# A mixed attention and feed-forward chain on one core: a scaling and half of a rounding moved from DVE to ACT, and all four engines' orders planned anew

## Chip, cores and metric

One NeuronCore of a Trainium2 chip runs the whole program in one launch. The metric is the device time of one execution in microseconds; lower is better. Half a per cent, 1.6 us, is about what a measurement of this kernel can tell from no change.

## The reference

The input x has 2 sequences of 512 tokens with 128 features; the context has 77 tokens for each sequence. Four layers follow each other, and every one adds to x:

```python
x = x + tanh(g_xattn[0]) * xattn0(layernorm(x), ctx, mask)     # 16 heads of 8
x = x + tanh(g_ffn[0])   * relu_mlp(layernorm(x))              # 128 -> 512 -> 128
x = x + tanh(g_xattn[1]) * xattn1(layernorm(x), ctx)           # one key and value head
x = x + tanh(g_ffn[1])   * (top-2 of 16 experts + shared expert)(layernorm(x))
x = x + tanh(g_xattn[2]) * xattn2(layernorm(x), ctx)
x = x + tanh(g_ffn[2])   * (one of 32 experts)(layernorm(x))
x = x + tanh(g_xattn[3]) * slots3(layernorm(x), ctx)           # 3 passes of slot attention + GRU
x = x + tanh(g_ffn[3])   * int8_product(layernorm(x), rhs)
```

In slots3 each pass takes scores of the tokens against the 77 keys, a softmax over the tokens (so each key's row has a sum over 512 tokens), divides by the sum over the keys, multiplies by the values, and feeds a GRU cell. In the last product every token's row is scaled by 127 / max|row| and rounded to integers.

## The kernel before

The two sequences are called halves (b = 0 and 1); half 2 in the code is preparation of weights and keys that both share. The work is cut into some 850 steps: ("pe", "scores", 1, 2, 0) is TensorE's part of the scores of half 1, layer 2, chunk 0. A step of one phase runs on PE (TensorE), ACT (ScalarE), DVE (VectorE) or POOL (GpSimd), and its followers wait for it by semaphores. Half 0 runs ahead of half 1, so that one half's matmuls fill the time in which the other half waits for ACT or DVE.

The order of the steps on each engine is fixed before the launch. `schedule()` is a list planner: it takes, again and again, the step with the lowest rank, which is its earliest possible time by the step times written in `prepare_steps` and `half_steps`, plus an offset of its own from the table `LATER`, minus a share of the work that still hangs on it. The same planner deals out the 8 PSUM banks of 512 columns, and puts spare matmuls into gaps that it sees on PE (`IDLE_FILLERS`, function `keep_warm`, 0.22 us each; their product is never read). In rows these fillers are `psum<-halves 128x512` (early on `psum<-wide 128x512`). Both kernels start with 13 more of them.

Names that the steps of this text touch:

- Attention layers: `maxima` (PE products of 32 rows into 4 banks, then DVE `TENSOR_REDUCE mx`), `max_rows` (four transposes and an ACT copy to `mx_t`), `scores` (PE into 4 banks, three products in parts hi and lo and one with `mx_t`; then four ACT exponentials into `wide`), `sums` and `values` (products with 32 columns: `wide,heads_of` and `wide,v_cols`), `sum_rows`, `spread`, `project`.
- PE works in three ways: whole (128x128), rows (32 rows: `maxima`, `scores`) and columns (32 columns: `sums`, `values`). The planner counts 0.095 us where the way changes (`SWITCH`).
- Slot passes: `slots_turn`, `slot_products`, `slot_scores` (DVE maximum, then ACT exponential with its sum over tokens), `slot_inverse` (reciprocal of the sum, then 78x386 value rows times it), `gru` (four products `wide 78x386`, each followed by a DVE reciprocal L1857 and L1858), `gru_r`, `gru_z`, `gru_end` (L1864, L1865, L1870, L1874, L1875 on DVE; three tanh and an Identity on ACT), `hidden`.
- The end: `integers` (row maximum L1578, scale, reciprocal L1580, four roundings L1582), `turn` of stage 7 (transposes, ACT L1373, clipping L1891), `quantised` (L1898, L1902), and the output's DMA.

Two lines of the slot pass before:

```python
                link(V.reciprocal(nmax[0:CTX, b, 2:3], nmax[0:CTX, b, 1:2]))
                V.tensor_scalar(vw_s[0:KEYS, b, :], vw[0:KEYS, b, :], nmax[0:KEYS, b, 2:3], None, ALU.mult)\
```

Of the kernel before, what the change touches and what calls it, by code (L numbers as in the profile page):

```python
# [7 lines left out]
ALU = mybir.AluOpType  # L8
ACT = mybir.ActivationFunctionType
# [6 lines left out]
P = 128  # L16
# [3 lines left out]
T = S // P  # L20
# [121 lines left out]
def first_columns(name, k):  # L142
# [49 lines left out]
}  # L192


# [1825 lines left out]
```

## Time and profile before

| | |
|---|---|
| median of 3 runs | 322.0 us (321.52 to 323.16) |
| the profiled execution | 322.01 us |
| its span | 320.2 us |
| busy: PE, DVE, ACT, POOL | 302.7, 231.3, 140.5, 60.2 us |
| instructions: PE, DVE, ACT, POOL | 2118, 642, 294, 83 |
| shares of the chain that ended last | PE 71%, DVE 19%, ACT 7%, issue 2% |

The span runs from the first to the last instruction that the profile shows; 1.8 us of the execution lie around it. Busy time of PE holds the fillers too, so a full PE is not yet a PE that does useful work. A time in a row is counted from the span's start.

### The profile page before, as it was taken

The page shows a single profiled execution, that of the slowest core. Times are in us where ns is not written, and L with a number is a line of the kernel's source. Part 1 is how long each engine was busy: PE and PEld are TensorE (multiplying, and loading weights), DVE is VectorE, ACT ScalarE, POOL GpSimd, SP SyncE. Part 2 cuts the span into 40 slices and gives each one's busy share as a digit, 9 for nine tenths or more (in the row PEclk, how much of TensorE's full clock was granted, in tenths as well). Part 3 has the DMA queues.
Part 4 walks back from the last instruction along what each step waited for, and adds up shares of the span by engine and source line. Part 5 has one row for each costly group of instructions (what it writes and reads, how often), then busy time and mean ns, then how long its engine had stood idle before and what let it go on. Part 6 is the DMA issues. An engine that isn't in the chain of part 4 may idle for free.

```text
span 320.2 us, 5732 instructions
## 1 busy us (share of the span) xinstructions
PE 302.7 (95%) x2118; PEld 202.6 (63%) x2118; DVE 231.3 (72%) x642; ACT 140.5 (44%) x294; POOL 60.2 (19%) x83
## 2 busy tenths in 40 slices
PE   8899999998899999999999999999999998899983
PEld 3463553883445478888788356479879874676441
DVE  4996864779866486878776485376457668999995
ACT  1337365234547462342424637513335636666300
POOL 6217631344001001003030301010210401001210
PEclk9999999999999999999999999999999999999998
DMA  6950220003100000000000000000000000000002
GB/s 177 320 201 0 72 74 2 0 3 85 60 0 2 2 0 0 3 0 2 0 2 0 1 3 2 0 2 0 0 2 0 2 1 2 0 1 2 0 1 66
DMA packets 8976, 8.73 MB, mean 27 GB/s; under 512 B 3547, under 2 KB 6901, under 8 KB 8949
## 3 DMA queue, kind: packets, MB, share of 16 engines
q1 hardware_dynamic: 8949, 8.37, 8.8%
q8 instruction: 17, 0.28, 0.4%
q14 instruction: 10, 0.08, 0.1%
HBM read 7.84 MB, written 0.52 MB: 26 GB/s over the span
## 4 chain that ended last, share of the span: by engine, by line
PE 71%; DVE 19%; ACT 7%; issue 2%; DVEq 0%; ACTq 0%
PE psum L974 65%; DVE mx L1695 4%; DVE wide L1858 2%; PE psum L1065 2%; ACT wide L1373 1%; ACT wide L1511 1%; DVE xn L1568 1%; PE psum L1103 1%; DVE xn L1875 1%; DVE wide L1865 1%; PE psum L1159 1%; ACT q L1373 1%; DVE xn_t L1874 1%; DVE wide L1864 1%; ACT wide L1501 1%
## 5 line engine op out<-in xcount | busy, mean ns | idle before, releaser
L913 POOL TENSOR_TENSOR nw<-mv,minus_half 128x2 f32<-128x2 f32 x32 | 22.5, 716 | 157.3 <-DVE mv L1562 157.3
L1373 ACT ACTIVATE wide<-psum 128x512 f32<-128x512 f32 x72 | 36.9, 614 | 11.6 <-PE psum L974 11.5
L1695 DVE TENSOR_REDUCE mx<-psum 128x4 f32<-128x308 f32 x96 | 38.6, 471 | 4.5 <-PE psum L974 4.3
L1373 ACT ACTIVATE q<-psum 128x512 f32<-128x512 f32 (+1 forms) x36 | 21.0, 594 | 27.2 <-PE psum L974 19.1
L974 PE MATMUL psum<-q_hi,first_hi 128*128 128x512 f32 (+1 forms) x68 | 31.6, 464 | 0.0
L974 PE MATMUL psum<-halves 128*128 128x512 bf16 x123 | 30.5, 379 | 0.5 <-ACT wide L1373 0.5
L974 PE MATMUL psum<-wide 78*128 78x386 f32 (+1 forms) x70 | 25.7, 503 | 3.1 <-DVE wide L1846 1.5
L974 PE MATMUL psum<-q_hi,first_lo 128*128 128x512 f32 (+1 forms) x68 | 26.9, 395 | 0.0
L974 PE MATMUL psum<-q_lo,first_hi 128*128 128x512 f32 (+1 forms) x68 | 26.8, 394 | 0.0
L974 PEld LDWEIGHTS psum<-early,wide 128*128 128x128 f32 x192 | 24.2, 192 | 1.4 <-DVE wide L1858 0.2
L974 PE MATMUL psum<-early,wide 128*128 128x128 f32 x192 | 24.7, 276 | 0.0
L974 PEld LDWEIGHTS psum<-w_ffn,wide 128*128 128x128 f32 (+1 forms) x176 | 22.8, 191 | 1.9 <-issue 0.4
L974 PE MATMUL psum<-w_ffn,wide 128*128 128x128 f32 (+1 forms) x176 | 23.4, 276 | 0.0
L974 PE MATMUL psum<-w_attn,q 128*128 128x128 f32 x176 | 22.8, 278 | 0.1
L974 PEld LDWEIGHTS psum<-w_attn,q 128*128 128x128 f32 x176 | 21.1, 192 | 1.3 <-issue 0.6
L1568 DVE TENSOR_SCALAR xn<-x,mv,nw 128x128 f32<-128x128 f32 x64 | 19.3, 351 | 2.6 <-POOL nw L913 1.4
L974 PEld LDWEIGHTS psum<-halves 128*128 128x128 bf16 x123 | 11.7, 98 | 13.0 <-issue 3.0
L974 PE MATMUL psum<-wide,v_cols 128*32 128x512 f32 x144 | 18.9, 598 | 0.5 <-DVE mx L1695 0.5
L974 PEld LDWEIGHTS psum<-wide 78*128 78x128 f32 (+1 forms) x70 | 11.2, 170 | 12.5 <-issue 5.2
L974 PE MATMUL psum<-wide,heads_of 128*32 128x512 f32 x144 | 18.9, 602 | 0.1
L1770 DVE TENSOR_TENSOR wide<-q,psum 128x512 f32<-128x512 f32 (+1 forms) x22 | 14.6, 683 | 5.8 <-ACT q L1373 4.4
L1373 ACT ACTIVATE wide<-psum,cols 128x512 f32<-128x512 f32 x12 | 8.2, 686 | 22.9 <-PE psum L974 22.8
(230 smaller groups left out, 551.7 us busy)
## 6 DMA issues: line engine op xcount, KB each, us to landing
early<-in_ffn SPq DMA_DIRECT2D x8, 256.0 KB, 3.1
w_attn<-in_attn SPq DMA_DIRECT2D x1, 640.0 KB, 7.7
w_attn<-in_attn SPq DMA_DIRECT2D x2, 288.0 KB, 6.5
x<-in_x SPq DMA_DIRECT2D x2, 256.0 KB, 3.8
w_ffn<-in_ffn SPq DMA_DIRECT2D x1, 512.0 KB, 7.0
early<-in_ffn SPq DMA_DIRECT2D x1, 512.0 KB, 3.9
out<-x SPq DMA_DIRECT2D x2, 256.0 KB, 2.3
rows<-in_rows SPq DMA_DIRECT2D x1, 468.0 KB, 6.2
```

The costliest lines, as they stand in the source:

```text
L913: G.tensor_tensor(nw[:, b, 2, tiles], mv[:, b, tiles, 1], minus_half[:, tiles], ALU.pow)\
L974: return nc.tensor.matmul(out_, lhs, rhs, start=start, stop=stop, **kw)
L1065: last = nc.tensor.transpose(bk[:, t * P:(t + 1) * P], (y if stage == 7 else xn)[:, b, t, :], ident)
L1103: last = nc.tensor.transpose(bk[:, t * P:(t + 1) * P], mx[:, b, t, :], ident)
L1159: last = nc.tensor.transpose(bk[:, t * P:(t + 1) * P], rinv_d[:, b, t, :], ident)
L1373: A.activation(dst, banks.bank(*name)[0:rows_, 0:cols_], fn, **kw).then_inc(drained["act"], 1)
L1501: last = A.activation(sq[:, b, t, :], slots[:, b, t, :], ACT.Square, accum_out=nw[:, b, 1, t:t + 1])
L1511: A.activation(ex[0:CTX, b, :], banks.bank("s", it, b)[0:CTX, :], ACT.Exp, bias=nmax[0:CTX, b, 0:1], accum_out=nmax[0:CTX, b, 1:2]).then_i ...
L1568: last = V.tensor_scalar(xn[:, b, t, :], x[:, b, t, :], mv[:, b, t, 0:1], nw[:, b, 2, t:t + 1], ALU.subtract, ALU.mult)
L1695: last = V.tensor_reduce(mx[:, b, t, lane_heads(g)], banks.bank("max", layer, b, t, g)[:, 0:GK].rearrange("p (h k) -> p h k", k=CTX), AX.X ...
L1770: V.tensor_tensor(wide[0:r, b, at_, :], act_s[k % 2][0:r, b, :], banks.bank("up", b, k)[0:r, :], ALU.mult)\
L1858: V.scalar_tensor_tensor(gates[:, b, t, :], u[:, 0:3 * D], inverse, gates_h[:, b, t, :], ALU.mult, ALU.add)\
```

## The change

There are three parts, and nothing that is computed changes. First, in each of the three slot passes of each half DVE now makes only the reciprocal of the sums; the product of the 78x386 value rows with it is an ACT instruction (Copy with a scale per row). Second, `integers` keeps the maximum, the scale and the reciprocal; of the four roundings DVE does two (`rounded`) and ACT two (`rounded_too`, Identity with scale and a bias column `up_col`). Third, many of the planner's step times are set to other values, the new steps are entered, and all of `LATER` is new, so the order changes on every engine and banks and fillers are dealt anew. There are 132 planned fillers before and 121 after, apart from the first 13.

```diff
 LATER = {
-        0: (-551, -416, -535, -47, 889, -2602, 967, -314, -617, 1, -552, 896, -357, 917, -128, -516, 122, -37, 171,
+        0: (-596, -35, 98, 416, 1125, 1176, 214, 74, 1060, 6, -9, 1305, 979, 1329, -4, -228, 1361, -242, 1426, 183,
...
-            step("integers", after=[at("dve", "norm_end", stage, 1)], dve=2.1)
+            step("integers", after=[at("dve", "norm_end", stage, 1)], dve=0.85)
+            step("rounded", after=[at("dve", "integers")], dve=0.65)
+            step("rounded_too", after=[at("dve", "integers")], act=0.6)
...
-                 then={"dve": in_order("dve", "maxima", layer, t)}, pe=0.25 if layer else 0.88, dve=1.53)
+                 then={"dve": in_order("dve", "maxima", layer, t)}, pe=0.38 if layer else 0.95, dve=1.53)
...
-            step("scores", layer, j, after=ready + in_order("pe", "scores", layer, j), pe=0.95 if layer else 1.95, act=1.95)
+            step("scores", layer, j, after=ready + in_order("pe", "scores", layer, j), pe=1.08 if layer else 2.0, act=1.95)
...
-                     + in_order("pe", phase, layer, j), pe=0.86, **evicted)
+                     + in_order("pe", phase, layer, j), pe=0.96 if phase == "sums" else 0.87, **evicted)
...
-        step("slot_inverse", it, after=[at("act", "slot_scores", it), prepared("act", "slots_in", 3)], dve=0.5)
+        step("slot_inverse", it, after=[at("act", "slot_scores", it), prepared("act", "slots_in", 3)], dve=0.2, act=0.5)
...
+            def rounded_too(b):
+                act.wait_ge(inverse_ready[b], 1)
+                for t in range(T // 2, T):
+                    A.activation(y[:, b, t, :], xn[:, b, t, :], ACT.Identity, bias=up_col[:, :], scale=route_s[:, b, 4, t:t + 1])\
+                     .then_inc(y_too_ready[b], 1)
...
+            def slot_inverse(b, it):
+                act.wait_ge(sums_inverted[b], it + 1)
+                if it:
+                    act.wait_ge(*banks.full("u", it - 1, b, T - 1))
+                A.activation(vw_s[0:KEYS, b, :], vw[0:KEYS, b, :], ACT.Copy, scale=nmax[0:KEYS, b, 2:3]).then_inc(vw_ready[b], 1)
...
-                link(V.reciprocal(inverse, scale))
-                for t in range(T):
+                V.reciprocal(inverse, scale).then_inc(inverse_ready[b], 1)
+
+            def rounded(b):
+                inverse = route_s[:, b, 4, :]
+                dve.wait_ge(inverse_ready[b], 1)
+                for t in range(T // 2):
...
-                link(V.reciprocal(nmax[0:CTX, b, 2:3], nmax[0:CTX, b, 1:2]))
-                V.tensor_scalar(vw_s[0:KEYS, b, :], vw[0:KEYS, b, :], nmax[0:KEYS, b, 2:3], None, ALU.mult)\
-                 .then_inc(vw_ready[b], 1)
+                V.reciprocal(nmax[0:CTX, b, 2:3], nmax[0:CTX, b, 1:2]).then_inc(sums_inverted[b], 1)
```

Three places of the orders follow. First TensorE in layer 1's attention, where half 0 turns from layer 0's feed-forward to the new attention: `early,wide` is the last product of `down0`, `consts,xn` a `turn`, `xn_t,w_attn` the `query`, `keys_hi,q_hi` the `maxima`, `consts,mx` the `max_rows`. Before:

```order
L974 MATMUL psum<-early,wide 128x128 x8
L1065 MATMUL psum<-consts,xn 128x128 x4
L974 MATMUL psum<-halves 128x512 x3
L974 MATMUL psum<-xn_t,w_attn 128x512
L974 MATMUL psum<-halves 128x512 x3
L974 MATMUL psum<-keys_hi,q_hi 128x308 x4
L974 MATMUL psum<-halves 128x512
L974 MATMUL psum<-keys_hi,q_hi 128x308 x4
L974 MATMUL psum<-halves 128x512 x4
```

And now:

```order
L983 MATMUL psum<-early,wide 128x128 x4
L1077 MATMUL psum<-consts,xn 128x128 x4
L983 MATMUL psum<-early,wide 128x128 x4
L983 MATMUL psum<-xn_t,w_attn 128x512
L983 MATMUL psum<-halves 128x512 x3
L983 MATMUL psum<-keys_hi,q_hi 128x308 x4
L983 MATMUL psum<-halves 128x512 x2
L983 MATMUL psum<-keys_hi,q_hi 128x308 x4
L983 MATMUL psum<-halves 128x512 x6
```

The last product of half 1's `down0` now stands behind the `turn`, where three fillers stood. Further on, `scores` chunks 0 and 1 of half 0 now follow each other with one filler between them, where a `maxima` of half 1 and a filler stood between them; the two fillers ahead of chunk 0 are gone, and half 0's `max_rows` comes ahead of half 1's first `maxima`. Up to the second chunk of scores 22 fillers stood here before and 19 stand now.

Second, TensorE in layer 2's attention, half 1, at the last two chunks of its `scores` (`q_lo,keys_hi` to `mx_t,minus_max`). Before:

```order
L974 MATMUL psum<-q_lo,keys_hi 128x512 x4
L974 MATMUL psum<-q_hi,keys_hi 128x512 x4
L974 MATMUL psum<-q_hi,keys_lo 128x512 x4
L974 MATMUL psum<-mx_t,minus_max 128x512 x4
L974 MATMUL psum<-halves 128x512 x4
L974 MATMUL psum<-q_lo,keys_hi 128x512 x4
```

And now:

```order
L983 MATMUL psum<-w_attn,q 128x128 x4
L983 MATMUL psum<-q_lo,keys_hi 128x512 x4
L983 MATMUL psum<-q_hi,keys_hi 128x512 x4
L983 MATMUL psum<-q_hi,keys_lo 128x512 x4
L983 MATMUL psum<-mx_t,minus_max 128x512 x4
L983 MATMUL psum<-wide,heads_of 32x512 x4
L983 MATMUL psum<-q_lo,keys_hi 128x512 x4
```

The four fillers are gone; a `sums` product stands in their place, and half 0's `project` (`w_attn,q`) moved from ahead of chunk 0 to between chunks 0 and 1.

Third, ACT in a slot pass (half 1's gates at L1522 to L1527, half 0's exponential at L1511). Before:

```order
L1522 ACTIVATE wide<-wide 128x512
L1526 ACTIVATE wide<-wide 128x512
L1527 ACTIVATE wide<-wide,half_col 128x512
L1532 ACTIVATE xn_t<-wide 128x512
L1511 ACTIVATE wide,nmax<-psum,nmax 77x512
L1516 ACTIVATE wide<-psum 128x4x128 x2
```

And now:

```order
L1546 ACTIVATE wide<-wide 128x512
L1550 ACTIVATE wide<-wide 128x512
L1551 ACTIVATE wide<-wide,half_col 128x512
L1540 ACTIVATE wide<-psum 128x4x128
L1529 ACTIVATE wide,nmax<-psum,nmax 77x512
L1556 ACTIVATE xn_t<-wide 128x512
L1536 ACTIVATE wide<-vw,nmax 78x386
L1540 ACTIVATE wide<-psum 128x4x128
```

L1536 is the new product with the inverse sums. The tanh of `gru_end` (L1532, now L1556), which followed the gates at once, now stands behind one `hidden` eviction (L1540) and the other half's exponential. DVE's order in the passes is almost the same, without L1846.

## Rows read from the trace of the kernel before

**Rows 1.** The page's busy times and TensorE's granted clock in 40 slices

```profile
PE 302.7 (95%) x2118; PEld 202.6 (63%) x2118; DVE 231.3 (72%) x642; ACT 140.5 (44%) x294; POOL 60.2 (19%) x83
PEclk9999999999999999999999999999999999999998
```

**Rows 2.** Windows: start:end and length, then busy us of each engine

```profile
71.26:90.00 18.74, 15.82 (x116) 6.94 (x113) 16.69 (x46) 9.45 (x21) 3.86 (x5) 1.00 0.23 62
90.00:196.38 106.38, 105.46 (x779) 75.11 (x779) 75.33 (x218) 48.08 (x88) 11.06 (x13) 1.00 0.00 1
...
249.99:320.00 70.01, 59.83 (x349) 39.37 (x346) 59.24 (x155) 30.58 (x80) 10.02 (x16) 0.98 0.03 9
```

**Rows 3.** Timeline of PE, layer 1: start, us, instruction, idle before

```profile
71.26 0.81 PE L974 MATMUL psum<-halves 128*128 128x512 bf16 x3
...
83.17 0.50 PE L974 MATMUL psum<-q_lo,keys_hi 32*128 32x512 f32 x4
...
96.06 0.60 PE L1103 MATMUL psum<-consts,mx 128*128 128x128 f32 x4
```

**Rows 4.** Timeline of DVE, layer 1

```profile
90.59 0.16 DVE L1656 TENSOR_SCALAR p_small<-p_ss 77x2 f32<-77x2 f32 x1
...
93.17 1.07 DVE L1647 TENSOR_TENSOR v_cols<-psum,consts 128x256 f32<-128x256 f32 x3
```

**Rows 5.** Timeline of PE, layer 2

```profile
186.57 0.38 PE L974 MATMUL psum<-halves 128*128 128x512 bf16 x1
187.20 0.76 PE L974 MATMUL psum<-pn_t,w_attn 128*128 128x154 f32 x4 [0.26 <-DVE mx L1695]
...
196.38 1.04 PE L974 MATMUL psum<-halves 128*128 128x512 bf16 x4
197.69 0.51 PE L974 MATMUL psum<-q_lo,keys_hi 32*128 32x512 f32 x4 [0.27 <-ACT wide L1373]
```

**Rows 6.** Timeline of PE, products of 32 columns and what follows them

```profile
200.29 1.04 PE L974 MATMUL psum<-wide,heads_of 128*32 128x512 f32 x8
201.15 1.04 PE L974 MATMUL psum<-wide,v_cols 128*32 128x512 f32 x8
202.12 1.08 PE L974 MATMUL psum<-early,xn_t 128*128 128x32 f32 x8
```

**Rows 7.** Timeline of DVE, slot passes

```profile
260.05 0.16 DVE L1845 RECIPROCAL nmax<-nmax 77x1 f32<-77x1 f32 x1
...
275.36 0.16 DVE L1845 RECIPROCAL nmax<-nmax 77x1 f32<-77x1 f32 x1 [0.24 <-ACT wide L1511]
275.56 0.42 DVE L1846 TENSOR_SCALAR wide<-vw,nmax 78x386 f32<-78x386 f32 x1
275.89 0.68 DVE L1836 SCALAR_TENSOR_TENSOR wide<-psum,hidden_bias 128x512 f32<-128x512 f32 x1
...
283.22 0.69 DVE L1829 TENSOR_REDUCE nmax<-psum 77x1 f32<-77x512 f32 x1 [0.30 <-PE psum L1323]
```

**Rows 8.** Timeline of PE, the first `gru` product of pass 1, half 0

```profile
260.81 5.42 PE L974 MATMUL psum<-wide 78*128 78x386 f32 x16 [0.61 <-DVE wide L1846]
```

**Rows 9.** Timeline of ACT: an eviction of 78x384, one tile of 128, stage 7

```profile
190.54 0.49 ACT L1373 ACTIVATE vw<-psum 78x384 f32<-78x384 f32 x1 [2.18 <-PE psum L974]
...
278.24 0.29 ACT L1501 ACTIVATE wide<-xn 128x128 f32<-128x128 f32 x1
...
309.88 0.69 ACT L1373 ACTIVATE nothot_t<-psum,round_col 128x512 bf16<-128x512 f32 x1 [6.48 <-PE psum L1065]
```

**Rows 10.** Timeline of DVE, the end

```profile
308.37 0.18 DVE L1580 RECIPROCAL route_s<-route_s 128x4 f32<-128x4 f32 x1
308.58 0.88 DVE L1582 TENSOR_SCALAR wide<-xn,route_s 128x128 f32<-128x128 f32 x4
309.37 1.24 DVE L1568 TENSOR_SCALAR xn<-x,mv,nw 128x128 f32<-128x128 f32 x4
310.67 0.29 DVE L1891 TENSOR_SCALAR nothot_t<-nothot_t 128x512 bf16<-128x512 bf16 x1
```

More of the change, by code:

```diff
@@ L246, in prepare_steps @@
     at = of(PREPARATION)
-    step("keys_in", 0, pe=0.3, act=0.3, dve=1.66, pool=1.7)
+    step("keys_in", 0, pe=0.3, act=0.3, dve=2.3, pool=1.7)
     step("mask_parts", dve=0.9)
@@ L254, in prepare_steps @@
         step("keys_in", layer, after=[at("pe", "keys_in", layer - 1)], then={e: [at(e, "keys_in", layer - 1)] for e in ("act", "dve", "pool")},
-             pe=0.3, act=0.33, dve=1.22, pool=1.7)
+             pe=0.3, act=0.33, dve=1.9, pool=1.7)
     step("out_bias", act=0.1)
@@ L297, in turn @@
         if stage == 7:
-            step("turn", stage, after=[at("dve", "integers")], pe=0.44, act=0.55, dve=0.25)
+            step("turn", stage, after=[at("dve", "rounded"), at("act", "rounded_too")], pe=0.44, act=0.55, dve=0.25)
     def bias(stage):
@@ L310, in attention @@
         step("query", layer, after=[at("act", "turn", stage)], then={"act": [prepared("act", "keys_in", 0)]},
-             pe=0.86, act=0.58, dve=0.65)
+             pe=0.98, act=0.55, dve=0.65)
         for t in range(T):
@@ L332, in attention @@
         step("project", stage, layer, after=[at("dve", "spread", layer)], then={"dve": [at("pool", "bias", stage)]},
-             pe=0.88, dve=0.65)
+             pe=0.98, dve=0.65)
         norm(stage + 1, [at("dve", "project", stage, layer)])
@@ L364, in half_steps @@
         step("weigh", c, after=[at("act", "weights_turn"), prepared("act", "slots_in", 0)] + in_order("pe", "weigh", c),
-             then={"dve": [at("dve", "up", SHARED + c)]}, pe=0.23, dve=0.7)
+             then={"dve": [at("dve", "up", SHARED + c)]}, pe=0.23, dve=0.63)
         down("down1", c, C1, [at("dve", "weigh", c)])
@@ L387, in half_steps @@
         step("slot_products", it, after=[at("act", "slots_turn", it), prepared("dve", "slots_in", 3)],
-             then={"dve": [at("pool", "square", it)]}, pe=0.92, dve=0.39)
+             then={"dve": [at("pool", "square", it)]}, pe=0.98, dve=0.39)
         step("slot_scores", it, after=[at("dve", "slot_products", it)], then={"act": [at("pool", "slot_rows")]},
@@ L395, in half_steps @@
                  **{reader: 0.54 if i < 2 else 0.6})
-        step("slot_inverse", it, after=[at("act", "slot_scores", it), prepared("act", "slots_in", 3)], dve=0.5)
+        step("slot_inverse", it, after=[at("act", "slot_scores", it), prepared("act", "slots_in", 3)], dve=0.2, act=0.5)
         for t in range(T):
-            step("gru", it, t, after=[at("dve", "slot_inverse", it)] + in_order("pe", "gru", it, t),
+            step("gru", it, t, after=[at("act", "slot_inverse", it)] + in_order("pe", "gru", it, t),
                  then={"dve": [at("act", "hidden", it, 1), at("dve", "hidden", it, 2)] + in_order("dve", "gru", it, t)},
@@ L406, in half_steps @@
     turn(7)
-    step("quantised", after=[at("dve", "turn", 7), prepared("dve", "slots_in", 4)], pe=0.25, dve=1.83)
+    step("quantised", after=[at("dve", "turn", 7), prepared("dve", "slots_in", 4)], pe=0.5, dve=1.83)
 def schedule():
@@ L684, in program @@
         round_col = sb("round_col", [P, 1])
+        up_col = sb("up_col", [P, 1])
         zeros16 = sb("zeros16", [P, P], BF16)
@@ L797, in program @@
         xn_ready = per_half("xn_ready")
+        inverse_ready = per_half("inverse_ready")
+        sums_inverted = per_half("sums_inverted")
+        y_too_ready = per_half("y_too_ready")
         q_hi_ready = per_half("q_hi_ready")
@@ L947, in _ @@
             G.memset(round_col[:, :], -ROUND)
+            G.memset(up_col[:, :], ROUND)
             G.memset(zeros16[:, :], 0.0)
@@ L1063, in turn @@
                 for t in range(T):
-                    pe.wait_ge(xn_ready[b], T * stage + t + 1)
+                    if stage == 7 and t >= T // 2:
+                        pe.wait_ge(y_too_ready[b], t + 1 - T // 2)
+                    else:
+                        pe.wait_ge(xn_ready[b], T * stage + t + 1)
                     last = nc.tensor.transpose(bk[:, t * P:(t + 1) * P], (y if stage == 7 else xn)[:, b, t, :], ident)
@@ L1537, in _ @@
                     "choose": choose, "down2": down2, "square": square, "slots_turn": slots_turn, "slot_scores": slot_scores,
-                    "hidden": hidden, "gru_r": gru_r, "gru_z": gru_z, "gru_end": gru_end, "split": split, "parts": parts}
+                    "hidden": hidden, "gru_r": gru_r, "gru_z": gru_z, "gru_end": gru_end, "split": split, "parts": parts, "slot_inverse": slot_inverse,
+                    "rounded_too": rounded_too}
             for phase, b, args in ORDERS["act"]:
@@ L1903, in quantised @@
                                        flat(x[:, b, :, :]), ALU.mult, ALU.add).then_inc(x_final[b], 1)
-            mine = {"norm": norm, "norm_end": norm_end, "integers": integers, "keys_in": keys_in, "mask_parts": mask_parts, "values_in": values_in,
+            mine = {"norm": norm, "norm_end": norm_end, "integers": integers, "rounded": rounded, "keys_in": keys_in, "mask_parts": mask_parts, "values_in": values_in,
                     "out_bias": out_bias, "slots_in": slots_in, "query": query, "maxima": maxima, "sum_rows": sum_rows, "spread": spread,
```

86 rows, old and new, of the table LATER are left out of this document.

## The prediction

> **What bounds the kernel now.** I read the page's busy times first: PE is busy for 95% of the span, and its granted clock is full in all but the last slices [rows 1]. That does not yet say that useful work of PE is the bound, since fillers count as busy. The windows by stage show three regimes [rows 2]. In 90 to 196 us PE is busy for 105.46 of 106.38 us with hardly a filler in it: there PE's own work sets the time, and whatever brings PE to 90 us with less work left is kept. In 71.26 to 90.00, layer 1's attention, PE shows 15.82 of 18.74 us, but 22 fillers stand in it; three of them took 0.81 us [rows 3] and four 1.04 [rows 5], so one more costs 0.22 and 22 cost 4.8 us. Useful work is 11.0 us of 18.74, and 7.7 are lost. DVE is busy for 16.69 of these 18.74 us. The third regime is 249.99 to the end: DVE 59.2 of 70.0 us, ACT 30.6, and PE padded with 95 fillers. In DVE's timeline of the slot passes one instruction follows the other almost without a gap; the gaps that I use are 0.24 and 0.30 us [rows 7].
>
> The profiled execution took 322.01 us and the median is 322.0, so one sum does for both; the 1.8 us around the span are left as they are.
>
> **Slot passes, the product moved to ACT.** Six DVE instructions L1846 go and six ACT ones come. Where DVE is the bound, one L1846 is worth its start to the next start, 275.56 to 275.89 = 0.33 us, and the 0.20 us from the reciprocal's start to it shrinks by some 0.03 [rows 7]. Three of them lie where DVE has no gap (pass 2 of half 1, pass 3 of both halves; I call the passes 1 to 3): 3 x 0.36 = 1.1 us less. The one of pass 1, half 0, lies under PE's work before 249.99 and is worth nothing. The two of pass 1, half 1, and pass 2, half 0, stand next to each other in a wait: from the reciprocal's start to PE's product it took 260.05 to 260.81 = 0.76 us [rows 7, 8]. ACT has not run this instruction; the nearest row is an eviction of 78x384, 0.49 us [rows 9]. With it the path is 0.16 + 0.05 + 0.49 + 0.15, about 0.9, the two hops being estimates from the gaps between such rows: 0.15 us more, once. From below, a product as quick as the 0.29 of 128 columns [rows 9] would gain 0.05 here; from above, the 0.69 of 512 columns with a bias [rows 9] loses 0.35. I take 0.49, whose size is the same to two columns.
>
> So the trace has 0.42 us for the product on DVE and 0.49 for the nearest one on ACT [rows 7, 9]: the move costs latency wherever the product is waited for, and gains only where DVE itself is the queue. The Trainium skill, "ScalarE: Activation LUTs", section "Rules for kernel authors", speaks against it: a multiplication belongs on VectorE, and an ACTIVATE is budgeted at 0.3 us and 0.83 ns per element. By that the product takes 0.62 us, an estimate from that page, and the sum below would be higher by 0.13.
>
> ACT's queue is the second price. In the new order the tanh of `gru_end` stands behind the other half's exponential, and DVE's `gru_end` waits for it. Set out with the durations of the trace, that tanh comes just when DVE is ready for it in pass 2 of half 1, and about when DVE comes to it in the next two. It fits without a margin. On the other side `slot_scores` of half 0, pass 3, now stands ahead of one `hidden` product on PE, which takes away the wait of 0.30 us at 283.22 [rows 7]: 0.3 less.
>
> **The end.** Two of four roundings go to ACT in each half. Four took 308.58 to 309.37, so two are 0.4 us of DVE [rows 10]. In half 1 that is on DVE's chain, and `quantised` of half 0 covers ACT's part: 0.4 less. In half 0 the clip L1891 came 2.30 us behind the reciprocal (308.37 to 310.67 [rows 10]). DVE would now be there after 1.85, but the path through ACT is 0.18 for the reciprocal, two tiles at 0.29, about 0.45 for the transposes, 0.69 for the eviction and 0.2 of hops: 2.1 [rows 9, 10], only 0.2 less. The tail in sum: +0.15 - 1.1 - 0.3 - 0.4 - 0.2 = **-1.85 us**. Its ends: -0.3, if ACT's order eats what the passes gain, and -2.4.
>
> **Layer 1, the new order.** One product of `down0` takes the place of three fillers, so 0.66 us hold useful work. On DVE the q_lo of half 0, one instruction of 0.7 us, moves behind half 0's last maximum, which so comes earlier by 0.3 us after the later start of half 1's norm. With the fillers ahead of the first scores gone these start at 82.2 to 82.5 where 83.17 stood [rows 3]. The next two chunks no longer take turns with half 1's maxima for the banks. Together I put PE 1.5 us ahead at 96 us, a fifth of the 7.7 us lost. Against it stands `slots_in`, 90.59 to 93.17 = 2.6 us of small DVE instructions [rows 4], which now run ahead of half 1's last three maxima. The transposes of these came at 96.06, 5 us behind 90.59 [rows 3, 4]; so the delay costs nothing unless PE is more than 3 us ahead. Term **-1.5**, ends 0 and -2.5.
>
> **Layer 2, the new order.** From the filler at 186.57 to 187.20 PE did nothing useful for 0.63 us, and from 196.38 to 197.69 for 1.31 us [rows 5]. Now products stand there; `project` moved behind scores chunk 0, so ACT starts its exponentials about 1 us earlier and is past them when the `sums` come. Term **-1.8** of 1.94, ends -0.6 and -1.9. Half 0's `project` is later by 1 us, and the turn that hangs on it later still.
>
> **Changes of PE's way.** A group of 32-column products went on to its like after 0.86 us (200.29 to 201.15) and to a whole-array product after 0.97 (201.15 to 202.12) [rows 6]: 0.11 for a change. I count 78 changes in PE's old order and 84 in the new (layer 0: 22 and 24, layer 1: 26 and 24, layer 2: 30 and 36). Six are **+0.7**, since layer 2 has no waits that hide them; ends +0.4 and +0.8. The Trainium skill, "TensorEngine Tiling (Array Packing)", section "Tiling Modes", says that a change of tiling mode drains TensorE. The trace agrees, with 0.11 us.
>
> **New waits.** The full stretch 90 to 196 lost 0.9 us to gaps [rows 2]. Over a third of PE's 352 steps stand elsewhere now, and no row of before can show a new wait: **+0.5**, half of what stands there, ends 0 and +2. The other edits (a column constant on POOL, semaphores, splits of weights moved by two places) lie under the work of PE and DVE; uncovered they would cost 0.1 to 0.3.
>
> Sum: 322.0 - 1.85 - 1.5 - 1.8 + 0.7 + 0.5 = 318.05, so **318.1 us**.
>
> **Rivals.** (1) The front gives nothing: half 1's maxima, late by `slots_in`, or half 0's `project` of layer 0, now behind two more chunks of scores, turn into waits of PE in the full stretches. It decides if PE gets more than 3 us ahead by 96 us, or if the next turn in layer 0 comes more than 0.5 us late. Then the front is worth 0 to -1.5, and the time is 320.2 to 321.7. For it: layer 0's slack is small by the durations; against it: the 5 us in layer 1 [rows 3, 4]. (2) The other side: ACT's queue decides the slot passes. A tanh of `gru_end` queued behind two more instructions of the size of 0.69 [rows 9] is later by 1.4 us, and DVE has one `hidden` eviction of 0.6 to put in. At 0.8 us for each of four passes the tail is +3.2 in place of -1.85, which gives 323.2; with a third of the front's gain lost too, 324. For it: the order of ACT; against it: ACT was busy for 30.6 of 70 us [rows 2] and ends up near 35. (3) All of layer 1's and 2's gain and no new wait: 316.3 or less.
>
> **The chances.** The forecast, tail and front both, 0.70: 316.3 to 320.4. Rival 1: 0.18, from there to 323.6, most of it below 321.7. Rival 2: 0.09. Rival 3: 0.03. The range that leaves out 2 in 10 is 316.3 to 321.3. Faster by over 0.5% (below 320.4): 0.73; within 0.5%: 0.18; slower: 0.09.
>
> **What would show it.** PE's first transposes of the slot passes for half 1, at the end of 249.99, should come 1.5 to 3 us earlier. The start of the first scores of layer 1, 83.17, should be 82.2 to 82.5. In the passes DVE should go from the reciprocal L1874 straight to its next instruction, with no wait for ACT ahead of `gru_end`; such waits over 1 us in sum tell rival 2. Idle time of PE between 90 and 196 above 2 us tells rival 1. The prediction is wrong too if TensorE's clock falls in the passes, where fewer fillers stand, or if the fillers ahead of the last turns (44 and 2) still run when their turn is ready.

## The result and the profile after

| | before | after |
|---|---|---|
| median | 322.08 us (321.52 to 323.16) | 320.06 us (319.80 to 320.13) |
| the profiled execution, its span | 322.01, 320.2 us | 320.13, 318.3 us |
| busy: PE, DVE, ACT, POOL | 302.7, 231.3, 140.5, 60.2 us | 301.7, 226.9, 145.5, 59.8 us |

The ratio is 0.9941, with an interval of 0.9922 to 0.9959; five more rounds gave 320.13 us and 0.9940 (0.9927 to 0.9954). The change made the kernel faster by 1.9 us. The forecast was 318.1, so 3.9 us less. The measured time lies in its range, but only half of the forecast gain came.

The page after, busy times and granted clock, as [rows 1]:

```profile
PE 301.7 (95%) x2107; PEld 200.9 (63%) x2107; DVE 226.9 (71%) x632; ACT 145.5 (46%) x304; POOL 59.8 (19%) x84
...
PEclk9999999999999999999999999999999999999999
```

The windows after, as [rows 2]; the last begins with DVE's `back` of half 1, the instruction that closes the experts' network ahead of the slot layer:

```profile
72.05:90.00 17.95, 16.09 (x123) 7.10 (x121) 16.10 (x53) 7.31 (x14) 3.76 (x5) 1.00 0.23 65
90.00:196.38 106.38, 105.51 (x780) 74.19 (x772) 75.19 (x206) 48.85 (x90) 10.83 (x13) 1.00 0.00 1
249.15:318.33 69.18, 58.46 (x341) 38.69 (x339) 56.63 (x146) 36.15 (x96) 10.15 (x16) 1.00 0.03 9
```

The clock is full throughout. In the last window DVE has 2.6 us less to do than in [rows 2] and ACT 5.6 more, but from that `back` to DVE's last product only 0.8 us are gained (below): DVE is idle there for 1.8 us more than before.

**Where the time went.** I follow single instructions through both traces and take their differences. DVE's last `back` of half 1 came at 250.24 and comes at 249.15, and DVE's last product at 316.71 and 314.84, so 1.1 of the 1.9 us come before this `back` and 0.8 in the passes and the end behind it. On PE, layers 1 and 2, as [rows 3, 5]:

```profile
72.05 1.10 PE L983 MATMUL psum<-xn_t,w_attn 128*128 128x512 f32 x2
...
83.34 0.51 PE L983 MATMUL psum<-q_lo,keys_hi 32*128 32x512 f32 x4 [0.51 <-ACT mx_t L1385]
...
195.64 1.07 PE L983 MATMUL psum<-wide,heads_of 128*32 128x512 f32 x8
196.64 0.50 PE L983 MATMUL psum<-q_lo,keys_hi 32*128 32x512 f32 x4
```

The 1.31 us without useful work at 196.38 of [rows 5] are gone; `sums` follow the scores at once. In layer 1 the first scores start at 83.34, not at 82.2 to 82.5, and they wait 0.51 us for ACT. Yet by DVE's `project` of layer 1 there is a gain: 100.50 became 100.20. Both numbers have to be read against the start. The first scores of layer 0 stood at 20.00 and stand at 20.32; counted from them the kernel is 0.6 us ahead there, and 0.6 behind (35.91 against 35.34) where PE starts the first feed-forward network, at the end of layer 0's attention. Layer 0 is a stretch on which the forecast had put no loss but two changes of way. The 0.3 us of the start vary from execution to execution. The 13 fillers at the start come 0.43 us apart at first and 0.22 apart later, and the moment of this step differs: the query behind them starts at 9.62 here, and at 8.09 in a second trace of the same kernel, where PE shows, for the seven fillers from 3.70 on and the next two products,

```profile
3.70 1.81 PE L983 MATMUL psum<-wide 128*128 128x512 bf16 x7
5.35 0.42 PE L983 MATMUL psum<-ctx_t,early 128*128 128x154 f32 x2
```

and in the first trace

```profile
3.70 3.19 PE L983 MATMUL psum<-wide 128*128 128x512 bf16 x7
6.69 0.62 PE L983 MATMUL psum<-ctx_t,early 128*128 128x154 f32 x2
```

The granted clock reads 1.00 in both; what sets the moment is not shown.

The slot passes on DVE, as [rows 7], at two of the six reciprocals:

```profile
258.97 0.16 DVE L1874 RECIPROCAL nmax<-nmax 77x1 f32<-77x1 f32 x1 [0.91 <-ACT wide L1529]
259.23 0.69 DVE L1865 SCALAR_TENSOR_TENSOR wide<-psum,hidden_bias 128x512 f32<-128x512 f32 x1
260.94 0.17 DVE L1884 RECIPROCAL route_s<-psum 128x1 f32<-128x1 f32 x1 [1.02 <-PE psum L983]
...
274.48 0.16 DVE L1874 RECIPROCAL nmax<-nmax 77x1 f32<-77x1 f32 x1 [0.24 <-ACT wide L1529]
274.56 0.67 DVE L1865 SCALAR_TENSOR_TENSOR wide<-psum,hidden_bias 128x512 f32<-128x512 f32 x1
```

PE's first product behind the reciprocal of 274.48, as [rows 8], and two more that wait for ACT:

```profile
275.62 1.54 PE L983 MATMUL psum<-wide 78*128 78x386 f32 x4 [0.40 <-ACT wide L1536]
...
284.53 2.18 PE L983 MATMUL psum<-wide 78*128 78x386 f32 x6 [0.76 <-ACT wide L1536]
...
294.25 2.83 PE L983 MATMUL psum<-wide 78*128 78x386 f32 x8 [0.35 <-ACT wide L1536]
```

ACT at the same place and at the two roundings of half 0, as [rows 9]:

```profile
274.87 0.61 ACT L1536 ACTIVATE wide<-vw,nmax 78x386 f32<-78x386 f32 x1
...
307.11 0.88 ACT L1462 ACTIVATE wide<-xn,up_col,route_s 128x128 f32<-128x128 f32 x2 [5.37 <-DVE route_s L1605]
308.41 0.69 ACT L1385 ACTIVATE nothot_t<-psum,round_col 128x512 bf16<-128x512 f32 x1 [0.42 <-PE psum L1077]
```

DVE does go from the reciprocal straight on, as forecast. But from the reciprocal's start to PE's product it takes 274.48 to 275.62 = 1.14 us, where the trace before had 0.76 at this place too (275.36 to 276.12), and the product on ACT takes 0.61, not 0.49. Where ACT is free the way is 0.95 us (behind the reciprocals of 258.97 and 293.30), close to the 0.9 of the forecast. At 274.48 and 283.39 the product also stands behind a tanh of `gru_end` in ACT's queue and starts 0.39 us behind the reciprocal's start:

```profile
283.25 0.62 ACT L1556 ACTIVATE xn_t<-wide 128x512 f32<-128x512 f32 x1
283.77 0.61 ACT L1536 ACTIVATE wide<-vw,nmax 78x386 f32<-78x386 f32 x1
```

Part of what DVE saves returns as a wait for PE's products (1.02 at 260.94, where it was 0.57 at 261.83) or as PE's own. DVE's row at 289.05 has such a wait, and with the product on DVE it is gone:

```profile
289.05 0.48 DVE L1852 TENSOR_TENSOR wide<-psum,nw 128x308 f32<-128x308 f32 x1 [0.39 <-PE psum L983]
```

The Trainium skill, "ScalarE: Activation LUTs", section "Rules for kernel authors", had 0.62 for the product by its budget of 0.3 us and 0.83 ns per element: the trace agrees with the page, and not with the eviction that I chose.

The end on DVE, as [rows 10]:

```profile
306.90 0.18 DVE L1605 RECIPROCAL route_s<-route_s 128x4 f32<-128x4 f32 x1
307.11 0.48 DVE L1611 TENSOR_SCALAR wide<-xn,route_s 128x128 f32<-128x128 f32 x2
307.51 1.24 DVE L1593 TENSOR_SCALAR xn<-x,mv,nw 128x128 f32<-128x128 f32 x4
309.20 0.29 DVE L1918 TENSOR_SCALAR nothot_t<-nothot_t 128x512 bf16<-128x512 bf16 x1 [0.46 <-ACT nothot_t L1385]
...
312.76 0.28 DVE L1918 TENSOR_SCALAR nothot_t<-nothot_t 128x512 bf16<-128x512 bf16 x1
```

From the reciprocal to the clip of half 0 it is 2.30 us, as before: the clip comes no earlier for the rounding shared with ACT. In half 1 DVE's part is 0.4 us shorter.

### The profile page after: what moved, and what is told of

The parts are those of the page before. It is cut to its first block, busy times and chain, and to the rows that moved or that the text cites. A ratio compares the mean times of both kernels' runs of the same rounds, so it can differ in the third digit from the quotient of the medians.

```text
span 318.3 us, 5713 instructions
## 1 busy us (share of the span) xinstructions
PE 301.7 (95%) x2107; PEld 200.9 (63%) x2107; DVE 226.9 (71%) x632; ACT 145.5 (46%) x304; POOL 59.8 (19%) x84
## 4 chain that ended last, share of the span: by engine, by line
PE 69%; DVE 20%; ACT 6%; issue 2%; POOL 1%; DVEq 0%; ACTq 0%
PE psum L983 63%; DVE mx L1724 5%; PE psum L1077 2%; DVE wide L1885 2%; ACT wide L1385 1%; DVE wide L1892 1%; DVE wide L1891 1%; ACT q L1385 1%; PE psum L1115 1%; ACT L1385 1%; ACT xn_t L1556 1%; DVE stats L1584 1%; DVE xn L1902 1%; PE psum L1163 1%; DVE xn_t L1901 1%
## 5 line engine op out<-in xcount | busy, mean ns | idle before, releaser
L983 PE MATMUL psum<-halves 128*128 128x512 bf16 x111 | 27.2, 379 | 0.0
L983 PEld LDWEIGHTS psum<-halves 128*128 128x128 bf16 x111 | 10.5, 98 | 12.0 <-issue 2.8
```

The costliest lines, as they stand in the source:

```text
L983: return nc.tensor.matmul(out_, lhs, rhs, start=start, stop=stop, **kw)
```

## The experiments

The passes are numbered 1 to 3, as in the prediction; where an expectation says pass 0, it is pass 1 (the code's `it == 0`). All kernels that keep "the new order" keep its planner's tables and so the place of every step; an edit taken back is taken back inside the step.

**The two edits taken back, one by one and both.** The diff of the first is below; in the second the loop of `rounded` runs over all four tiles and `rounded_too` is empty; the third has both.

```diff
 def slot_inverse(b, it):            # ACT
-    act.wait_ge(sums_inverted[b], it + 1)
-    ...
-    A.activation(vw_s[0:KEYS, b, :], vw[0:KEYS, b, :], ACT.Copy, scale=nmax[0:KEYS, b, 2:3])
+    pass
 def slot_inverse(b, it):            # DVE
-    V.reciprocal(nmax[0:CTX, b, 2:3], nmax[0:CTX, b, 1:2]).then_inc(sums_inverted[b], 1)
+    link(V.reciprocal(nmax[0:CTX, b, 2:3], nmax[0:CTX, b, 1:2]))
+    V.tensor_scalar(vw_s[0:KEYS, b, :], vw[0:KEYS, b, :], nmax[0:KEYS, b, 2:3], None, ALU.mult)
```

> The changed kernel with its order, and only the product of the value rows back on DVE, behind the reciprocal. Budget theory (as forecast: the slot passes are DVE's sum of work): DVE gets back three waited-for products of 0.36 us, so 1.1 us above the changed kernel's 320.06, 321.2. Loop theory (the passes go round DVE, ACT and PE, and the product on ACT with its handover took 1.14 us from reciprocal to PE where DVE took 0.76): what DVE saves is given back in waits, so 319.8 to 320.4.

Measured: 320.56 us, 0.9954 (0.9938 to 0.9969). The product on ACT is worth some 0.4 us, between the two theories and nearer to the loop theory than to the 1.1 of the forecast. The trace says where: from the `back` of half 1 to DVE's `slots_back` of half 1 (the instruction behind the last pass) it is 54.57 us here and 54.08 with the product on ACT, but the stretch up to the reciprocal of half 1's pass 2 is 0.2 us quicker here. (The profiled execution took 319.56 us, 1.0 less than the median of this kernel: its first scores came early, at 19.42, and a copy in layer 0 was short, of which more below. The stretches behind `back` are not touched by that.)

> The changed kernel with its order, and only the last rounding whole on DVE again. Forecast's terms: 0.6 us above the changed kernel's 320.06 (0.2 for half 0, 0.4 for half 1), 320.7. From the trace after the change: half 0's ACT roundings ended 0.46 us behind DVE's part, so nothing for half 0 and 0.4 for half 1: 320.45.

Measured: 320.62 us, 0.9956 (0.9942 to 0.9970): 0.5 above, all of it in half 1. From half 1's `integers` to its clip it is 3.75 us (309.61 to 313.36), where the changed kernel has 3.35 (309.41 to 312.76), and `integers` itself starts 0.2 later; the clip of half 0 stands at 309.2 in both. So the two roundings are worth the 0.6 of the forecast together, or nearly, though not by half 0's clip.

> The changed kernel's order with both edits undone (product and rounding on DVE). If the edits are worth what the forecast gave them (1.1 and 0.6), 321.8, that is the order brings 0.3 only. If the loop theory holds, the order carries nearly all: 320.4 to 320.7.

Measured: 320.89 us, 0.9965 (0.9954 to 0.9977). The order alone brings 1.1 us, and both edits on top 0.8. Neither expectation holds: the edits are worth half of what the forecast gave them.

**Layer 0 in the old order.** `SEQUENCE` below lists the steps of the kernel before as far as a cut, and from there the remaining ones in the new order; every engine follows it, and the banks are dealt anew in the same way.

```diff
-    while waiting:
+    for wanted in SEQUENCE:
+        waiting = [steps[keys[wanted]]]
```

The first cut is at half 0's `query` of layer 1, the second at the first `hidden0` of half 0.

> The changed kernel, with all steps up to the start of layer 1 in the order of the kernel before and the rest in the new order. If layer 0's new order costs what the traces show by its end (0.7 to 0.8 us), 319.3 to 319.5. If that lateness was of the one profiled run, or is swallowed by a wait in layer 1, 320.0.

Measured: 320.52 us, 0.9954 (0.9939 to 0.9968), 0.4 above the changed kernel. The trace points to the cause: with this cut PE runs six fillers (73.47, 1.46 us) ahead of layer 1's first maxima, which start 54.71 us behind the first scores, against 53.70 in the profiled execution of the changed kernel and 54.18 in its second trace. The cut also keeps the last product of `down0` ahead of half 0's turn, and so undoes what the new order had gained there. It was a badly placed cut and says little about layer 0. (The two effects were not separated.)

> The changed kernel, with every step up to the first matmuls of half 0's feed-forward network in the order of the kernel before, and from there the new order with its own fillers. In the traces the new order reaches these matmuls 35.91 us after layer 0's first scores, the old one 35.34. If layer 0 costs the new order this 0.57, 319.5. The rival: a later wait swallows it, 320.06.

Measured: 319.18 us, 0.9915 (0.9899 to 0.9931). That is 0.9 below the changed kernel. The first feed-forward product comes 35.44 us behind the first scores (35.91 in the changed kernel's first trace and 36.36 in its second; the reason for the two values comes below), and nothing later swallows it.

**Which engine's order it is in layer 0.** In the first of these only PE's order is set back (below), in the second only DVE's and POOL's (`keys_in` of layers 1 and 2 again ahead of half 1's `query`, not between `spread` and `project` of half 0).

```diff
 # PE, layer 0, half 1 (scores, sums) and half 0 (project)
 scores10,0
+project00
 scores10,1
-sums10,0
 scores10,2
-project00
+sums10,0
```

> The changed kernel with its orders on DVE, ACT and POOL, and only PE's order in layer 0 set back: the projection of half 0 between the first two score groups of half 1, and the first sums behind the third. If the two further changes of matmul shape on PE make most of layer 0's 0.57, 0.25 to 0.3 less, 319.8. If DVE's key and value preparation ahead of the projection makes it, PE gets to the projection earlier and waits there: 320.1 or more.

Measured: 320.33 us, 0.9942 (0.9927 to 0.9958): nothing gained. Two changes of matmul shape are gone, but PE then waits 0.75 us ahead of the third group of scores:

```profile
47.70 1.02 PE L1058 MATMUL psum<-mask_t,halves 77*128 77x512 bf16 x4 [0.75 <-ACT wide L1460]
```

In the old order one of these scores went to the bank that DVE's `project` had emptied. Now DVE is at the keys when PE has finished the projection, the bank stays taken, and the scores are dealt a bank that ACT has yet to empty.

> The changed kernel with its orders on PE and ACT, and DVE's and POOL's order of layer 0 set back (the keys of layers 1 and 2 made before half 1's query, not between the spread and the projection of half 0). If DVE's queue there is what layer 0 lost, 319.2 to 319.5. If it takes PE's and ACT's order with it, 320.0 or more: the pieces only fit together.

Measured: 320.59 us, 0.9953 (0.9940 to 0.9965): nothing gained here either; PE waits 0.47 us for `v_cols` and 0.89 for half 1's inverse sums on DVE. Each half of the old order alone meets a wait of the new one. What layer 0 loses by its order belongs to the order of the engines together, and I can name no single step for it.

**A copy that waits for POOL.** Counted from the first scores, kernels with the same order differ in layer 0 by 0.5 us: they reach the first feed-forward product after 35.90 to 35.94 us in three traces and 36.36 to 36.39 in five. DVE's timeline in the kernel with the rounding on DVE:

```profile
39.72 1.28 DVE L1727 COPY xn_t<-rinv 128x512 f32<-128x512 f32 x1
```

POOL in the same kernel:

```profile
38.23 2.49 POOL L940 TENSOR_TENSOR first_lo<-early,first_hi 128x512 fp32r<-128x512 f32 x2 [3.52 <-ACT first_hi L1441]
```

And DVE's copy in the changed kernel, where POOL's second subtraction started 0.6 us behind it:

```profile
40.20 0.43 DVE L1733 COPY xn_t<-rinv 128x512 f32<-128x512 f32 x1
```

The copy ends 0.28 us behind POOL's pair (40.72), and PE waits 0.97 us for it. It took 1.28 or 1.29 us in six traces (the five of 36.36 to 36.39, and the kernel with PE's order set back), each time with the pair's second subtraction running when the copy began. It took 0.43 in four, where the second subtraction began after it. In these four ACT, whose copy of the weights POOL needs, had waited 1.05 to 1.46 us for their load, and 0.28 at most in the traces with the long copy. So layer 0 loses about 0.6 us by its order and, in five of eight traces, 0.4 to 0.5 more by this copy. Together that is close to the 0.9 which the old order of layer 0 gave back. The old order is not free of it: the copy took 0.54 in the kernel before, 0.72 in the kernel with layer 0 set back, and 1.05 in the last kernel below. The Trainium skill, "SBUF — State Buffer", section "SBUF: two separate sides", describes a port pair that DVE and GpSimd lock against each other for a whole instruction. I tried a form of the copy that would not need it:

```diff
-    V.tensor_copy(rinv_d[:, b, :, :]..., each)
+    V.tensor_tensor(rinv_d[:, b, :, :]..., each, each, ALU.max)
```

> The changed kernel, with the copy that spreads the inverse sums over the head rows (512 columns, 0.43 us alone, 1.29 us in four of seven traces of the new order, each time with POOL at a subtraction until its end) written as a maximum of the row with itself, which gives the same values. If the copy waits for POOL and this form doesn't, it takes 0.6 to 0.7 us in every run, PE's wait of 0.97 us ahead of the second spread is 0.3 or less, and the median falls by 0.3 to 0.5 to 319.6 to 319.8. If the copy's length has another reason, 320.1.

Measured: 320.83 us, 0.9961 (0.9949 to 0.9973), a loss. The form waits as well:

```profile
39.76 1.55 DVE L1734 TENSOR_TENSOR xn_t<-rinv 128x512 f32<-128x512 f32 x1
```

POOL's pair ran from 38.27 to 40.77, and the form ended 0.54 us behind it. It is also the slower form where nothing is in its way: 0.69 us at the four places of layers 1 and 2, where the copy takes 0.43. The same page says that an operation with two inputs in SBUF takes the lock too; I had read past it, and the trace agrees.

**The edits in the old order.** PE and DVE keep the order of the kernel before; ACT gets the products one or two steps behind the exponentials, and the roundings.

> The kernel before with its order on PE and DVE, and only the two edits: ACT takes the product (one or two ACT steps behind the exponentials) and two of the four last roundings. By the forecast's terms 1.7 us below before, 320.3. By what the same edits were worth in the new order (0.3 to 0.5 for the product, 0.4 to 0.6 for the rounding) 321.2. If the passes' loop decides and ACT's handover falls on it, the product brings nothing or less: 321.5 or more.

Measured: 323.67 us, 1.0056 (1.0037 to 1.0076): slower than before by 1.8 us. This is the forecast's second rival in kind, ACT's queue decides, though it is the product that is queued and not the tanh. ACT in pass 2 of half 0 and its neighbour:

```profile
258.98 0.67 ACT L1577 ACTIVATE wide<-psum,nmax 77x512 f32<-77x512 f32 x1
...
259.64 0.68 ACT L1577 ACTIVATE wide<-psum,nmax 77x512 f32<-77x512 f32 x1
...
260.32 0.58 ACT L1588 ACTIVATE wide<-psum 128x512 f32<-128x512 f32 x1
...
260.80 1.12 ACT L1584 ACTIVATE wide<-vw,nmax 78x386 f32<-78x386 f32 x2
```

DVE there:

```profile
259.77 0.16 DVE L1922 RECIPROCAL nmax<-nmax 77x1 f32<-77x1 f32 x1 [0.17 <-ACT wide L1577]
...
263.08 0.17 DVE L1932 RECIPROCAL route_s<-psum 128x1 f32<-128x1 f32 x1 [1.41 <-PE psum L1031]
```

The reciprocal is there at 259.93, and the product begins at 260.80, behind the other half's exponential and an eviction of `hidden`. DVE then waits 1.41 us for PE. Of the 2.0 us lost by the end of the passes (DVE's `slots_back` of half 1 at 307.38, before 305.34), 0.1 are the start, 0.4 are lost before half 1's `back`, 0.8 here and 0.7 from half 1's pass 2 to its pass 3. The rounding still brings its 0.4.

> The two edits in the old order of PE and DVE, as in the run before, but with ACT's slot passes in the new order (the product of half 0 ahead of the exponentials of half 1 in pass 1, ahead of the last tanh in others). If the 1.8 us lost there is the product's place in ACT's queue, most of it comes back: 322.0 to 322.4. If DVE's and PE's order must move with it, 323.3 or more.

Measured: 325.16 us, 1.0099 (1.0084 to 1.0114). It got worse, so the new place in ACT's queue, taken alone, does not bring the time back. But 0.9 us more of it arose in layer 1, where nothing was to change: the banks had been dealt anew for this kernel, and `project` of layer 1 came later. In the passes it is 57.90 us against 56.68 from `back` to `slots_back` of half 1, 1.2 more.

**Is the product on the chain?**

> The changed kernel, with the product of pass 0 of both halves on DVE, those of passes 1 and 2 on ACT. From the trace with all products on DVE: pass 0 of half 0 was 0.15 to 0.2 us quicker with DVE and the later passes 0.5 slower. If the handover to ACT is what pass 0 pays, 319.8 to 319.9; if a product on DVE costs its 0.36 wherever it stands, 320.3 or more.

Measured: 320.00 us, 0.9933 (0.9918 to 0.9949), between the two and within the noise of the changed kernel. The trace has the passes 0.2 us shorter (53.89 against 54.08 to `slots_back`), as expected for the handover, but to DVE's last product it is 65.7 us in both.

```diff
-    mm(bk[:, 0:UPDATE], ex[...], vw_s[0:KEYS, b, :])
+    mm(bk[:, 0:UPDATE], ex[...], vw[0:KEYS, b, :])      # and the product on ACT left out
```

> The changed kernel without the product: the update matmuls read the value rows unscaled, so that the division by the key sums is left out. An upper bound for what taking the product off DVE could be worth. If the passes are bound by DVE's sum of work (forecast), the product on ACT is already free and this gives 320.0. If they are a chain over DVE, ACT and PE, ACT's 0.61 us and its handover stand in five or six of the six passes, and this gives 318.3 or less.

Measured: 318.52 us, 0.9891 (0.9876 to 0.9905), 1.6 below the changed kernel, and in it 54.08 became 52.78 us from `back` to `slots_back`. The kernel leaves out the division, so this is a bound and no kernel to use. DVE was rid of the product already in the changed kernel, so a bound by DVE's work would have shown nothing. With the product on ACT it stands on a chain over DVE, ACT and PE. With the product on DVE this run can't tell the chain from DVE's own time: leaving it out there is worth 2.0 us, and six times 0.36 are 2.2.

> The new order up to the first slot step, the old order from there, both edits undone. Against the new order with both edits undone (320.89, 0.35% under before) this shows what the new order is worth in the passes without the edits. The forecast gave it a loss of 0.15 us there, so 320.7; by the traces the new order's passes are 0.5 us shorter, so 321.4.

Measured: 321.42 us, 0.9975 (0.9963 to 0.9987), against 320.89 with the new order in the slot steps too. The difference of 0.5 (0.3 by the ratios) is not larger than the two intervals tell, and the traces do not put it where the expectation looked. (The forecast's +0.15 was the price of the handover to ACT; for the order it had -0.3.) DVE's `back` of half 1 in the kernel with the old slot order, and in the one with the new:

```profile
249.72 0.75 DVE L1850 SCALAR_TENSOR_TENSOR x<-q,gain,x 128x512 f32<-128x512 f32 x1 [2.67 <-ACT q L1429]
```

```profile
249.10 0.75 DVE L1803 SCALAR_TENSOR_TENSOR x<-q,gain,x 128x512 f32<-128x512 f32 x1 [2.13 <-ACT q L1382]
```

Half 0's `back` stands at 225.87 and 225.89 in them, so 0.6 us arise between the two, where half 0's first pass runs beside half 1's experts. From half 1's `back` to DVE's last product both take 66.6 us. That `slots_back` comes 0.6 us sooner in the new order is only a matter of where one looks: the new order puts half 0's `norm_end` (0.60 us) behind it. DVE before and after:

```profile
303.25 0.60 DVE L1568 TENSOR_SCALAR xn<-x,mv,nw 128x128 f32<-128x128 f32 x2
...
305.34 0.75 DVE L1881 SCALAR_TENSOR_TENSOR x<-xn,gain,x 128x512 f32<-128x512 f32 x1
```

```profile
303.23 0.75 DVE L1908 SCALAR_TENSOR_TENSOR x<-xn,gain,x 128x512 f32<-128x512 f32 x1
304.02 0.60 DVE L1593 TENSOR_SCALAR xn<-x,mv,nw 128x128 f32<-128x128 f32 x2
```

The traces of all these kernels, from half 1's `back` to the reciprocal of its pass 2 (274.48 in the changed kernel), and from there to DVE's last product, in us:

| kernel | `back` to reciprocal | reciprocal to last product |
|---|---|---|
| before | 25.13 | 41.35 |
| changed | 25.33 | 40.37 |
| product on DVE | 25.13 | 41.07 |
| rounding on DVE | 25.32 | 40.97 |
| both on DVE, new order | 25.14 | 41.45 |
| both on DVE, old slot order | 25.15 | 41.44 |
| product left out | 24.67 | 39.74 |

The second column holds the three products that the forecast counted. Their move to ACT gains 0.5 to 0.7 us there and costs 0.2 in the first column. Leaving the product out brings 0.6 us more in the second column, though DVE does the same work as in the changed kernel.

**The two gains together.**

> Layer 0 in the old order up to the first feed-forward matmuls, the rest in the new one, and pass 0's products on DVE. If the two gains add (0.9 and 0.1 below the changed kernel), 319.0 to 319.1; if pass 0's 0.2 is again lost in a wait of half 1, 319.2.

Measured: 318.85 us, 0.9911 (0.9885 to 0.9936). It beats the kernel before by 0.9% (2.9 us) and the changed one by 1.2 us; against the kernel with layer 0 alone set back (319.18) the difference is less than the intervals tell, so the second gain is not shown.

## Why the prediction was half right

The terms, against what the two traces show (first scores of layer 0 as the zero for layers 0 and 1, DVE's `back` of half 1 as the border of the passes):

| stretch | forecast | measured |
|---|---|---|
| start (differs from execution to execution) | 0 | +0.3 |
| layer 0 | +0.2 (two changes of way) | +0.6 |
| layer 1 | -1.5 - 0.2 | -1.2 |
| layer 2 and the experts, with new waits | -1.8 + 0.7 + 0.5 | -0.8 |
| passes and end | -1.85 | -0.8 |
| sum | -3.95 | -1.9 |

(The changes of PE's way are split by the forecast's count: two more in layer 0, two fewer in layer 1, six more in layer 2.)

**Layers 1 and 2** were right in mechanism and nearly in size. A product of `down0` did take the place of fillers, and the wait at 196.38 is gone. `slots_in` did not hold up PE: no wait for half 1's maxima shows, so the first half of rival 1 fell. PE was idle for 0.87 us between 90 and 196 (0.92 before), so the new waits of 0.5 us did not come in this stretch; what the changes of way cost was not measured apart. Half 1's `back` came 1.1 us earlier, where the forecast's sign was 1.5 to 3.

**Layer 0** is the term that was missing. The forecast saw that half 0's `project` moved behind two chunks of scores and named it in rival 1, but with no price below a delay of 0.5 us. The stretch lost 0.6, so this half of rival 1 came about, and the front's gain of 1.1 us lies in that rival's 0 to 1.5. In executions with the long copy it lost 1.0, and setting the four engines back there together gave back 0.9. Setting back PE alone, or DVE and POOL alone, gave back nothing. Why the pieces hold each other is shown for one bank and one wait only; the rest stays open.

**The passes** are the step that failed: "Three of them lie where DVE has no gap": 3 x 0.36 = 1.1 us less. DVE did save this work, as the windows show, but the three brought 0.5 to 0.7. Behind them DVE has new waits of 0.5 us (0.39 of them at 289.05), since PE gets the product later: ACT does it in 0.61 us with a handover on each side, 0.95 to 1.14 from the reciprocal to PE where DVE needed 0.76. So DVE's work was not the only bound. A chain that goes round DVE, ACT and PE bounds this stretch too, and the product on ACT is on it: left out, with DVE's work the same, it brings 0.6 us more here. The reading of a DVE "almost without a gap" was too kind as well: between half 1's `back` and `slots_back` the trace before has ten waits over 0.15 us, 4.6 us in sum, 0.7 of them from 275.36 on. The wait that was in the sum, at +0.15, came to 0.2 and was right. Taking the product away altogether is worth 1.6 us; giving it to ACT is worth 0.4 in all, where the forecast had 0.95.

The second term that failed here is the wait of 0.30 us at 283.22. It went, as forecast, but DVE waits 0.24 for ACT at the next reciprocal, and the new order from `back` to the end is 0.1 us longer than the old (66.58 against 66.47) and not 0.3 shorter. The rounding was right in size (0.5 to 0.6 us by time and trace, 0.6 forecast). In half 0 its clip came no earlier, since ACT's two tiles took 0.88 us and not 0.58.

**Rival 2** did not happen in the changed kernel, where DVE's waits for ACT ahead of `gru_end` stay at 0.27 us or less behind half 1's `back`. Its kind, ACT's queue as the bound, came when the edits were put into the old order (+1.8, against +3.2 in that rival), with the product in the tanh's place. The new order is worth 1.1 us by itself, all of it before half 1's `back`, and the edits are worth 0.8 in it, where they lost 1.8 in the old order with the places that I gave them on ACT. Whether other places would do better there stays open; the one other that I tried did not.

## What to carry over

Before work is moved off the busiest engine, ask whether that engine is full or is one station of a chain: leave the instruction out altogether for one run and look at what is gained. Where it is on the chain, the other engine's duration and two handovers count, and part of the saved time of the first engine comes back as its wait. An edit and its order are to be judged together, and a new order stretch by stretch: it may win in one layer and lose in another, and a splice can keep the better part of each. A stretch is to be measured between instructions that have the same work ahead of them in both orders.

## What was not expected of the hardware

- DVE's copy of 512 columns took 0.43 us, or 1.28 when POOL was in the middle of two subtractions, and a maximum of two SBUF operands 1.55; a cast of 154 columns took 0.23 and, in the same kernel at 43.4, beside POOL, 1.26.
- The first query of layer 0 on PE started between 8.09 and 9.65 us in the traces, at 8.09 and 9.62 in two of the same kernel, since the first fillers changed from 0.43 to 0.22 us apart at another moment. Two executions are to be compared from an instruction behind the start, not from zero.
- ACT scaled 78x386 from SBUF in 0.61 us, and evicted 78x384 from PSUM in 0.49 [rows 9]. The first takes a column as its scale and the second takes none; whether the column or the memory makes the difference was not tested.
